# Larger pacing weights for the layer-norm and mixing stage that runs between attention tiles in a fused attention and FFN kernel

## What is computed

```python
x_proj = (x @ w_in.T + b_in).reshape(b, l, h, -1)        # h = 16 heads
q, k, v = jnp.split(x_proj, 3, axis=-1)
att = jnp.einsum('blhd,bmhd->blmh', q, k) * scale
att = jax.nn.softmax(att, axis=2)
opt = jnp.einsum('blmh,blhd->blhd', att, v).reshape(b, l, d)
attn_out = opt @ w_out.T + b_out
...
xr = mu_r * x + (1.0 - mu_r) * x_prev                    # x_prev: x one position earlier
xk = mu_k * x + (1.0 - mu_k) * x_prev
r = jax.nn.sigmoid(xr @ W_r)
out = r * (jnp.square(jax.nn.relu(xk @ W_k)) @ W_v)
...
x = x + attn(layernorm(x))
x = x + ffn(layernorm(x))
```

## Time and profile before

| | |
|---|---|
| time before, median of 2 runs | 2479.64 us (2434.63 to 2524.64) |
| the profiled execution's own time | 2434.41 us |
| its span (slowest core, core 2) | 2432.9 us |
| spans of the eight cores | 2419.6 to 2432.9 us |
| busy: TensorE, ScalarE, VectorE | 1381.6, 1251.4, 770.5 us |
| ScalarE exponentials (L457) | 1024 of 1021 ns, 1036.0 us |
| ScalarE idle before them | 435.6 us, most of it behind TensorE's L439 |
| TensorE idle before L750 | 234.7 us, of which 233.2 behind VectorE's L732 |
| mean granted TensorE clock, core 2 | 0.801 |

### The profile page before, as it was taken

How to read it: one execution, slowest core, us unless ns; L and a number is a source line. 1 busy time by engine, 2 the same in 40 slices (tenths; PEclk the granted TensorE clock), 3 DMA queues, 4 the chain that set the end, 5 groups by cost and what they waited for, 6 DMA issues and landing times.

```text
span 2432.9 us, 22201 instructions; the slowest of 8 cores (2419.6 to 2432.9 us)
## 1 busy us (share of the span) xinstructions
PE 1381.6 (57%) x5875; PEld 453.8 (19%) x5984; DVE 770.5 (32%) x1500; ACT 1251.4 (51%) x2369; POOL 95.5 (4%) x182
## 2 busy tenths in 40 slices
PE   1466665556736673753346666664667366736635
PEld 0122221112212121220012222211212021212212
DVE  1711111341252126232762111125313521351362
ACT  0055558658837783700002665575688387746002
POOL 0000000000000000000000000000000000000000
PEclk9667777888969796896579677787889698968969
DMA  6011111323413350456025111122334134414515
GB/s 106 1 18 18 18 18 26 70 39 79 88 38 65 71 99 18 82 103 119 0 35 112 18 18 18 18 39 57 53 78 92 22 64 86 92 21 83 113 34 104
DMA packets 46873, 135.82 MB, mean 56 GB/s; under 512 B 5648, under 2 KB 5776, under 8 KB 46752
## 3 DMA queue, kind: packets, MB, share of 16 engines
q0 software_dynamic: 27424, 100.67, 25.1%
q1 hardware_dynamic: 19328, 33.72, 4.1%
HBM read 218.26 MB, written 16.78 MB: 97 GB/s over the span
## 4 chain that ended last, share of the span: by engine, by line
PE 44%; issue 19%; DVE 17%; DMA 10%; ACT 9%; DVEq 1%; ACTq 1%; POOL 0%; SPq 0%; POOLq 0%
PE sg L439 11%; PE pacc L349 9%; ACT e_scr L457 6%; PE pacc L789 6%; PE pacc L750 5%; PE pacc L534 5%; DMA xr_stage<-x_cm 5%; DMA qb<-x_cm 3%; DMA wbuf<-wpk 2%; PE pacc L582 2%; DVE ar L717 2%; DVE ar L703 2%; PE pacc L801 2%; ACT rt_scr L816 1%; DVE ar L672 1%
## 5 line engine op out<-in xcount | busy, mean ns | idle before, releaser
L457 ACT ACTIVATE e_scr<-sg 128x1024 bf16<-128x1024 f32 x1024 | 1036.0, 1021 | 435.6 <-PE sg L439 434.7
L439 PE MATMUL sg<-kb,qb 64*128 64x512 bf16 x2048 | 379.5, 452 | 417.1 <-ACT e_scr L457 417.1
L750 PE MATMUL pacc<-ar,wbuf 128*128 128x512 bf16 x493 | 133.0, 418 | 234.7 <-DVE prevc L732 233.2
L349 PE MATMUL pacc<-ln,wbuf 128*128 128x512 bf16 x1001 | 232.9, 394 | 11.9 <-DVE qb L392 6.9
L457 ACT ACTIVATION_READ_ACCUMULATOR e_scr<-sg 128x1 f32 x1024 | 205.7, 201 | 0.0
L789 PE MATMUL pacc<-ar,wbuf 128*128 128x512 bf16 x499 | 154.3, 461 | 84.7 <-ACT e_scr L457 46.3
L439 PEld LDWEIGHTS sg<-kb,qb 64*128 64x128 bf16 x2048 | 68.9, 97 | 692.9 <-issue 692.9
L156 POOL DMA_DIRECT2D wbuf<-wpk x176 | 93.6, 533 | 2318.5 <-PE sg L439 1045.6
L801 PE MATMUL pacc<-ar,wbuf 128*128 128x512 bf16 x496 | 131.0, 408 | 34.8 <-DMA wbuf<-wpk 32.7
L534 PE MATMUL pacc<-ln,wbuf 128*128 128x512 bf16 x492 | 127.1, 398 | 40.7 <-DVE opt L562 36.7
L813 ACT ACTIVATE rt_scr<-pacc 128x512 f32<-128x512 f32 x64 | 38.4, 600 | 206.0 <-PE pacc L789 206.0
(11 more groups left out here) (77 smaller groups left out, 1054.3 us busy)
## 6 DMA issues: line engine op xcount, KB each, us to landing
wbuf<-wpk POOLq DMA_DIRECT2D x176, 512.0 KB, 6.1
xr_stage<-x_cm SPq DMA_DIRECT2D x64, 256.0 KB, 5.6
out_cm<-out_stage SPq DMA_DIRECT2D x64, 256.0 KB, 3.8
qb<-x_cm POOLq DMA_DIRECT2D x2, 4096.0 KB, 36.3
ident_sb<-ident_in SPq DMA_DIRECT2D x1, 64.0 KB, 2.3
ones_sb<-ones_in SPq DMA_DIRECT2D x1, 32.0 KB, 1.8
indic_sb<-indic_in SPq DMA_DIRECT2D x1, 32.0 KB, 5.8
bqkv_sb<-bqkv SPq DMA_DIRECT2D x1, 12.0 KB, 9.8
```

What stands on the lines that cost most here:

```text
L349: lambda e, gq=gq, dcl=dcl, cc=cc, tt=tt, half=half: e.matmul(PA(half), wtile(gq, dcl, cc), ln[:, cc * 2048 + tt * 512: cc * 2048 + (tt + ...
L439: lambda e, p=p, lc=lc, mh=mh, n=n, r0=r0, g=g: e.matmul(sgs[g][:, n * 512:(n + 1) * 512], qb[r0:r0 + 64, p * 2048 + lc * 128: p * 2048 + ...
L457: lambda e, ab=ab, col=col, g=g, zt=zt: e.activation(e_scr[:, ab * 1024:(ab + 1) * 1024], sgs[g][:, :], AF.Exp, scale=float(SCALE), accum_ ...
L750: lambda e, gq=gq, dcl=dcl, cc=cc, pa=pa: e.matmul(PA(pa), wtile(gq, dcl, cc), ar6[:, cc * 512:(cc + 1) * 512], start=(cc == 0), stop=(cc ...
```

## The change

Only prices change, all of them in stage D. No instruction is added or removed, none changes its form or its operands.

```diff
@@ behind the two casts L660, L661
-                yield 1
+                yield 4
@@ in the normalizing loop (eight rounds), L677
-                    if cc == 3:
-                        yield 1
+                    if cc % 2 == 1:
+                        yield 3
@@ behind the differences, L698
-                yield 1
+                yield 6
@@ in the mixing loop (eight rounds), L730
-                    if cc % 3 == 2:
-                        yield 1
+                    if cc % 2 == 1:
+                        yield 4
@@ behind mixv, L736
-                yield 1
+                yield 8
```

## The result

The changed kernel takes 0.9854 of the time of the kernel before, 95% interval 0.9817 to 0.9891. The prediction was 2395 / 2434.41 = 0.9838. The profiled execution took 2400.95 us. Four of the changed kernel's twelve executions took 2435 to 2495 us, with one die at a lower granted clock; the ratios here leave such executions out, for both kernels.

A forecast was written before the change was run, and what follows sets the result against it. No single engine bounds it, but who waits for whom, notably TensorE before L750 for VectorE's L732. Terms -20.9, -8.2 and +9.2 sum to -19.9 us a sequence, -39.8 for both: 2434.41 to 2395 us, range 2363 to 2422.

The forecast's parts named there:

- Stage D keeps its length: Stage D takes 21 more tiles a sequence for nothing; L615 to L750 stays at 45 us.
- Rival 2: Stage D: tiles running beside VectorE's chain stretch it; at half more the time is 2478 us; chance 0.03.
- The tail of block 2: Block 2's stages E and F, now bare, take 67.60 us instead of 88.52: -20.9 us a sequence.
- Rival 3: Block 2's tail is dearer than its pattern, with TensorE at half clock throughout: 2457 us; chance 0.03.
- Four tiles that moved: One tile more in A, one in B, two in E, at 2.3 us each: +9.2 us a sequence.
- Stage F of blocks 0 and 1: With 49 tiles instead of 53 a sequence, stage F falls from 174.0 to 165.8 us: -8.2 us.
- The regular pairs: Stage F, a sequence: 3 pairs with one tile behind L789, two behind L801, at 9.36 us; 8 reversed at 10.65.
- 5 odd ones with 16 tiles: Stage F of blocks 0 and 1: a sequence's odd pairs, priced at 3.28 us a tile, 52.5 us.
- A rule on the clock: First L750 group behind stage D: the skill's rule would save 8 us in all; the prediction followed the trace instead.
- Rival 1: TensorE's clock comes back in first L750 groups (-8 us) and stage F's pairs (-25 us): 2362 us; chance 0.18.
- Within 2%: Whole kernel: a time between 2385.7 and 2483.1 us, given 0.73; faster 0.25, slower 0.02.

The follow-up runs named there:

- experiment 6: Kernel with stage F prices 0 and 16 and rate 32, its mixing loop split so L750 waits only for the xk rounds: 0.9369 of the kernel before.
- experiment 5: Changed kernel, stage F prices 0 and 16, stage D's last price 24 for 8: 0.9744 of before; last price 40 with rate 36: 0.9503.
- experiments 1 and 4: The first: kernel before with rate 27 at 24, so block 2's stages E and F go bare without filling D: 1.011 of before; the other: see experiment 4.
- experiment 4: Changed kernel, rate 27 raised: 30, 0.982 of before; 32, 0.9888; with stage F prices 0 and 16: 30, 0.9598; 32, 0.9451.

## Why the prediction was right, and where it was not

*Stage D keeps its length.* Right: 261.4 us for the six, against 266.0, with 21 tiles a sequence more in them; VectorE's chain took 27.3 us in both. ScalarE idles 10.4 to 11.4 us before the first exponential behind L750 in blocks 0 and 1, as forecast; block 2's two waits for L732, 13.3 and 13.5 us, lie above the 8 to 12 that the prediction named for all six. Rival 2 (a stretched chain) falls by that row. That it is VectorE that sets the length was argued from the wait for L732, and is shown by experiment 6; that there was slack is shown by experiment 5. The 4.6 us less belong to the two cores that were compared: in the mean of all eight cores the six take 262.4 us before and 261.8 after.

*The tail of block 2, -20.9 us a sequence.* Right: 88.5 to 66.6 us in the mean of the two sequences, against 67.6 in the bare stretches that the trace of before held. Over all cores the stages E and F of block 2 went from 93.4 to 73.9 us in the mean of 16. Rival 3 (a slow tail) falls: its clocks are 0.92 and 0.94.

*Four tiles that moved, +9.2 us a sequence.* The sign was right and the size too large, +12.0 for both sequences in place of +18.4: a tile costs 1.4 us in A, 0.1 to 1.4 in B, and 1.5 to 2.1 in E (experiments 1 and 4), not 2.3 in each.

*Stage F of blocks 0 and 1, -8.2 us a sequence.* Wrong: 0.0 on the slowest cores, -2.5 a sequence in the mean of all. The regular pairs were priced nearly rightly (9.42 and 10.85 us, against 9.36 and 10.65). The step that failed is "5 odd ones with 16 tiles", priced as 16 x 3.28. The four pairs with two tiles, one on either side of L801, took 9.45 to 9.94 us, not 2 x 3.28 = 6.6; they make 12.5 of the 16.4 us by which the four stages missed the sum. They were no faster than pairs with one tile ahead and two behind (9.42). So a pair is not priced by its tiles: behind L801 stands the chain over L813, L816, L818 and L826 to the next L789, and one tile covers only part of it. It is no fixed floor, for with the rate 32 such pairs took 7.7 to 9.9 us. The trace of before held one in each sequence (9.03 and 8.77 us), and an average over the stage hid them. The forecast for the whole stood in spite of this, since against the 16.4 us stand 6.4 that the moved tiles cost less, 2.0 more from the tail and 4.6 in stage D, with 2.9 lost in all else. That only 6.3 us of miss were left is in part luck.

*A rule on the clock.* The changed kernel bears out what I read from the trace of before: the tiles in stage D run 2.42 us apart, half clock, and the first L750 group behind each filled stage D takes 3.57 us for eight matmuls, against 1.90 for a later one. Rival 1 did not happen in the changed kernel, whose stages F have clocks of 0.76 to 0.88. Its mechanism exists: in block 0's stage F, first sequence, the clock is 0.80 in the changed kernel and 0.93 with the other pair order, the rate 32 and four tiles fewer (experiment 4).

*The chances.* "Within 2%" was the outcome, at 1.5%. What makes the gain a third of the wait is now measured and not only argued: the fill is worth 2.6%, the displacement costs 1.1%.

## What to carry to other kernels

Filling a stall with work from a shared budget is an exchange: price what the filler leaves bare, and look for a stretch of the same trace in which that work already runs bare. Do not price a stage by dividing its time by the units in it; look for the chain that a unit fewer does not shorten, and place the filler behind the instruction that the next group waits for. Prices that pace a generator are only sums. Between stage D's prices stand VectorE instructions alone, so by the condition of L855 the 43 added units in one `yield` ahead of L750 would give the same order on every engine; no kernel here was run that way.

## What was not expected of the hardware

The projections and first tiles of a sequence (L349, with L439 between) are the same instructions in every kernel here. They took 283.8 us on the slowest core of the changed kernel. In three of the other profiled executions they took 297.7 to 298.5 on the slowest core, at a lower granted clock, and each time on exactly two neighbouring cores (6 and 7, 2 and 3, 4 and 5), while the other six took 281.5 to 283.9. What sets it off is open. The first 282 us of that stretch on core 4 and on core 3 of the same execution of the kernel with the price 40 and the rate 36:

```profile
108.00:390.00 282.00, 192.81 (x747) 64.71 (x757) 45.91 (x112) 152.56 (x293) 4.25 (x8) 0.68 0.09 15
```

```profile
108.00:390.00 282.00, 184.22 (x780) 62.14 (x779) 45.90 (x112) 166.10 (x318) 4.24 (x8) 0.72 0.09 15
```

Core 4 got 293 ScalarE instructions done where core 3 got 318. Since the metric is the slowest of eight cores, one such stretch is 15 us of the result, as much as many of the terms above. Stage sums, taken over the cores, are the better measure of a small term than a time.
